# Feed-forward in pairs of tiles, half chunks turned as one, and norm, projection and merge joined to it

## The reference

```python
def fp4_quant_dequant(x):
    xb = x.reshape(shape[:-1] + (shape[-1] // BLOCK, BLOCK))
    scale = jnp.maximum(jnp.max(jnp.abs(xb), axis=-1, keepdims=True) / 6.0, 1e-12)
    idx = jnp.searchsorted(_MID, jnp.abs(xb / scale))
    return (_GRID[idx] * jnp.sign(xb / scale) * scale).reshape(shape)

def ffn(x, w_gate, w_up, w_down):                    # fp4_linear quantises both sides
    h = silu(fp4_linear(x, w_gate)) * fp4_linear(x, w_up)
    return fp4_linear(h, w_down)

x = x + 0.5 * ffn(layernorm(x), ...)
x = x + attention(layernorm(x), w_qkv, w_out)        # softmax(q k / 4) v, then w_out
x = x + 0.5 * ffn(layernorm(x), ...)
```

## Time and profile before

| | us |
|---|---|
| median of three runs | 4138.01 (4137.37 to 4140.72) |
| the profiled execution's own time | 4135.73 |
| its span, first to last instruction | 4133.9 |
| PE busy | 4009.2 (97%) |
| DVE busy | 3712.7 (90%) |
| ACT busy | 2450.9 (59%) |
| POOL busy | 1098.6 (27%) |

### The profile page before, as it was taken

One profiled execution on the slowest core, in us unless ns is written; L12 is line 12 of the kernel. 1 busy time (PEld: TensorE's weight loads), 2 busy tenths in 40 slices (PEclk: granted clock), 3 DMA queues, 4 the chain that ended last, 5 costly groups with the idle time before them and its releaser, 6 DMA issues. The chain is left out here.

```text
span 4133.9 us, 108840 instructions
## 1 busy us (share of the span) xinstructions
PE 4009.2 (97%) x46275; PEld 2314.2 (56%) x46275; DVE 3712.7 (90%) x6341; ACT 2450.9 (59%) x2770; POOL 1098.6 (27%) x1156
## 2 busy tenths in 40 slices
PE   3999998999999999999999999999999999899999
PEld 2777775568764444444444444444444443677776
DVE  7999983689999999999999999999999995799998
ACT  1222225467777777777777777777777778122222
POOL 3888872300000000000000000000000000288886
PEclk8999999999999999999999999999999999999999
DMA  3000002310010110001001001001100110100000
GB/s 134 1 1 1 1 1 99 122 58 29 21 40 20 30 31 29 21 27 34 25 25 34 26 21 39 21 29 31 29 21 29 31 29 5 34 16 16 16 16 21
DMA packets 77709, 125.57 MB, mean 30 GB/s; under 512 B 27688, under 2 KB 56744, under 8 KB 75432
## 3 DMA queue, kind: packets, MB, share of 16 engines
q1 hardware_dynamic: 77224, 118.62, 9.8%
HBM read 72.55 MB, written 36.31 MB: 26 GB/s over the span
## 5 line engine op out<-in xcount | busy, mean ns | idle before, releaser
L971 DVE TENSOR_REDUCE stats<-ps_b 128x1 f32<-128x512 f32 x4016 | 2488.7, 682 | 105.7 <-PE ps_b L1020 6.3
L958 ACT ACTIVATE probs<-ps_s 128x1024 f32<-128x1024 f32 x2048 | 1983.8, 1021 | 649.6 <-PE ps_s L1054 649.6
L1020 PE MATMUL ps_b<-w_ffn 96*32 96x512 bf16 x10688 | 1112.0, 382 | 6.2 <-PEq L653 5.9
L1032 PE MATMUL ps_o<-probs,w_qkvT 128*32 128x512 f32 x8192 | 1090.5, 592 | 0.6 <-ACT probs L958 0.6
L1054 PE MATMUL ps_s<-w_ffn 99*32 99x512 bf16 x10752 | 977.0, 380 | 0.5 <-ACT probs L958 0.5
L545 PE MATMUL ps_gu_f<-w_ffn,zT_f 128*128 128x352 f32 x2048 | 634.9, 463 | 10.3 <-DVE h_f L450 9.4
L1054 PEld LDWEIGHTS ps_s<-w_ffn 99*32 99x32 bf16 x10752 | 365.7, 98 | 377.4 <-issue 188.8
L1020 PEld LDWEIGHTS ps_b<-w_ffn 96*32 96x32 bf16 x10688 | 357.7, 96 | 376.7 <-issue 174.0
L1020 PE MATMUL ps_b<-K,Q 96*32 96x512 bf16 x5376 | 558.6, 381 | 0.2
L1054 PE MATMUL ps_s<-Q,K 99*32 99x512 bf16 x5632 | 508.8, 381 | 2.2 <-ACT probs L958 1.8
L545 PEld LDWEIGHTS ps_gu_f<-w_ffn,zT_f 128*128 128x128 f32 x2048 | 383.1, 192 | 204.8 <-ACT zT_f L402 11.9
(11 more groups left out here) (124 smaller groups left out, 3084.9 us busy)
## 6 DMA issues: line engine op xcount, KB each, us to landing
qk_parts_dram<-qk_parts SPq DMA_DIRECT2D x96, 256.0 KB, 2.9
w_ffn<-qk_parts_dram SPq DMA_DIRECT2D x84, 192.0 KB
w_ffn<-qk_parts_dram SPq DMA_DIRECT2D x84, 128.0 KB
x_res<-in_L_attn_x SPq DMA_DIRECT2D x4, 2048.0 KB, 19.6
factor<-denom_dram SPq DMA_DIRECT2D x64, 128.0 KB, 5.3
out<-x_res SPq DMA_DIRECT2D x16, 512.0 KB, 2.6
v_then_heads<-OT SPq DMA_DIRECT2D x224, 32.0 KB
w_ffn<-qk_parts_dram SPq DMA_DIRECT2D x84, 64.0 KB
```

Of the source, the lines that this page charges most:

```text
L958: nc.scalar.activation(probs[:, (2 * kt + half) % 4, :], ps_s[:, half, :], ACT.Exp, scale=float(DH) ** -0.5).then_inc(exped, 1)
L971: nc.vector.tensor_reduce(mx[:, s, k // 4, bass.ds(k % 4, 1)], ps_b[:, bank, :], AX.X, ALU.max).then_inc(bank_free, 1)
L1020: last = nc.tensor.matmul(ps_b[j:j + STRIP, bank, :], Q[s][0:PAIRS, qt * P + j:qt * P + j + STRIP], K[s][0:PAIRS, kb * 512:(kb + 1) * 512] ...
L1032: last = nc.tensor.matmul(ps_o[32 * c:32 * c + 32, :], V[s][:, kt, :], probs[:, (2 * kt + c // 2) % 4, (c % 2) * 512:(c % 2 + 1) * 512], s ...
```

## The change

In the feed-forward:

- Tiles are taken in pairs. hq and hT hold 2 x 704 = 1408 columns, 11 chunks without padding. Chunk 5 is shared: its rows 0 to 63 are the last 64 columns of the even tile, rows 64 to 127 the first 64 of the odd one. The even tile's h is turned as 5 chunks, the odd tile's as 6. The weights of the down product are laid out in 11 chunks to match, with five more pairs of transposes and copies in the weights stage and one small transfer.
- down(t) multiplies five whole chunks; for the odd tile two matmuls of 64 rows follow, one on each half of the array's rows, one into each tile's bank, and finish both tiles.
- LAG is 2. PE turns h of tile i-2 in step i, ahead of the gate/up products of tile i.
- On DVE the residual of tile i-3 now stands behind h of tile i, and for an even tile it waits for the down products of the odd tile after it; the statistics stand behind the block maxima.

Around it:

- The second norm is split: tiles 0 to 47 are done inside the first feed-forward (DVE behind steps 54 and 56, ACT behind step 55), and ACT prepares projection's first y there; tiles 48 to 63 are done inside projection. Projection starts with the q/k products of chunk 0, and turns chunk 1 only behind them.
- The merge is the head of the second feed-forward's block. It uses six banks of that stage. The norm of tiles 0 to 15 stands behind round 7, steps -4 to -1 of the feed-forward behind rounds 12, 15, 18 and 21, and the norm of the rest behind round 31.
- Several buffers share memory with others. Attention's instructions are the same.

```diff
-        AHEAD, LAG = 4, 3
+        AHEAD, LAG = 4, 2
...
+        def chunks(t):
+
+            return range(0, EVEN) if t % 2 == 0 else range(EVEN, PAIR)
...
-                    if old:
-                        dve.wait_ge(dn_done, i - LAG)
-                        nc.vector.scalar_tensor_tensor(out=m.x[:, i - LAG - 1, :], in0=ps_dn[:, q, 0:D], scalar=0.5 / SHRINK**2,
-                                                       in1=m.x[:, i - LAG - 1, :], op0=ALU.mult, op1=ALU.add).then_inc(x_done, 1)
...
-                    if old and out is None:
-                        dve.wait_ge(x_done, i - LAG)
-                        nc.vector.bn_stats(m.stats[:, i - LAG - 1, :], m.x[:, i - LAG - 1, :])
+                    if old:
+                        t = i - LAG - 1
+                        dve.wait_ge(dn_done, t + 2 - t % 2)
+                        nc.vector.scalar_tensor_tensor(out=m.x[:, t, :], in0=ps_dn[:, t % 2, 0:D], scalar=0.5 / SHRINK**2,
+                                                       in1=m.x[:, t, :], op0=ALU.mult, op1=ALU.add).then_inc(x_done, 1)
...
+                def turn_h(t):
+
+                    pe.wait_ge(hq_ready, t + 1)
+                    if t >= 1:
+                        pe.wait_ge(hT_kept, t)
+                    for k, c in enumerate(chunks(t)):
+                        last = nc.tensor.transpose(ps_hT[:, k * P:(k + 1) * P], hq[:, c * P:(c + 1) * P], m.ident[:])
+                    last.then_inc(hT_turned, 1)
+
+                def down(t):
+
+                    pe.wait_ge(hT_kept, t + 1)
+                    if t >= 2:
+                        pe.wait_ge(x_done, t - 1)
+                    whole = [c for c in chunks(t) if c != EVEN]
+                    for c in whole:
+                        last = nc.tensor.matmul(ps_dn[:, t % 2, 0:D], hT[:, c * P:(c + 1) * P], m.w_dnT[:, c, :],
+                                                start=(c == whole[0]), stop=False)
+                    if t % 2 == 1:
+                        for u in range(2):
+                            rows = slice(u * HALF_ROWS, (u + 1) * HALF_ROWS)
+                            last = nc.tensor.matmul(ps_dn[:, u, 0:D], hT[rows, EVEN * P:(EVEN + 1) * P], m.w_dnT[rows, EVEN, :],
+                                                    start=False, stop=True)
+                    last.then_inc(dn_done, 1)
...
+class NormAhead:
+
+
+    LO, HI = 0, 3 * KT
+    AT = HI + 6
...
+    def vector(self, dve, i):
+        if i == self.AT:
+            dve.wait_ge(self.norm.stats_in, self.HI)
+            self.norm.variance(dve, 0, self.LO, self.HI)
+        if i == self.AT + 2:
+            self.norm.finish(dve, 0, self.LO, self.HI)
...
+class Merge:
...
+    NORM_AFTER = PER_BATCH - 1
+    STEP_AFTER = {12: -4, 15: -3, 18: -2, 21: -1}
...
+    def wait_weights(self, pe):
+
+        pe.wait_ge(self.w_loaded, 16)
+        pe.wait_ge(self.x_done, self.NG)
```

More of the change, by code:

```diff
@@ L204, in weights_phase @@
         first_down = len(jobs)
[L205 to L207 removed]
+        for c in range(PAIR):
+            rows = P if c != EVEN else HALF_ROWS
+            lo = c * P if c <= EVEN else c * P - I
+            jobs.append(([dn3[:, j, lo:lo + rows] for j in range(KD)], m.w_dnT[0:rows, c, :], rows))
         with nc.Block() as block:
@@ L341, in ffn_phase, with normalise_chunk @@
+def normalise_chunk(nc, act, m, i):
+    for j in range(CHUNK):
+        t = i * CHUNK + j
+        last = nc.scalar.activation(m.y[:, j, :], m.x[:, t, :], ACT.Identity, bias=m.shift[:, t:t + 1], scale=m.rstd[:, t:t + 1])
+    last.then_inc(m.y_ready, 1)
+def ffn_phase(nc, m, tag, out, lead=None, tail=None):
     with ExitStack() as ctx:
@@ L417, in step @@
                         nc.scalar.activation(halves(silu[:]), gate, ACT.Silu, scale=1.0 / SHRINK).then_inc(silu_done, 1)
-                straight(step)
+                if lead is None:
+                    for i in range(-AHEAD, 0):
+                        at(step, i)
+                else:
+                    lead.scalar(act, lambda i: at(step, i))
+                for i in range(NT + LAG + 1):
+                    at(step, i)
+                    if tail is not None:
+                        tail.scalar(act, i)
             @block.vector
@@ L484, in step @@
                         nc.vector.tensor_tensor(hs[:, q, :], hs[:, q, :], hM[:, q, :], ALU.add).then_inc(h_step, 1)
-                straight(step)
+                if lead is None:
+                    for i in range(-AHEAD, 0):
+                        at(step, i)
+                else:
+                    lead.vector(dve, lambda i: at(step, i))
+                for i in range(NT + LAG + 1):
+                    at(step, i)
+                    if tail is not None:
+                        tail.vector(dve, i)
             @block.gpsimd
@@ L532, in step @@
                     if live(-LAG):
-                        pe.wait_ge(hq_ready, i - LAG + 1)
-                        if live(-LAG - 1):
-                            pe.wait_ge(hT_kept, i - LAG)
-                        for c in range(FC):
-                            last = nc.tensor.transpose(ps_hT[:, c * P:(c + 1) * P], hq[:, 1 - q, c * P:(c + 1) * P], m.ident[:])
-                        last.then_inc(hT_turned, 1)
+                        turn_h(i - LAG)
                     if live(0):
                         pe.wait_ge(zT_kept, i + 1)
+                        if first and lead is not None:
+                            lead.wait_weights(pe)
                         if live(-1):
@@ L655, in _, with high_part @@
             def _(act):
-                for i in range(-2, NC):
+                def high_part(i, q):
+                    if i >= 2:
+                        act.wait_ge(parts_stored[q], i // 2 * (16 * STORES))
+                    for n, (lo, hi) in enumerate(halves(i)):
+                        act.wait_ge(qk_done, i + n + 1)
+                        nc.scalar.copy(parts[q][0][:, lo:hi], ps_qk[:, lo:hi]).then_inc(high, 1)
+                        if i == END:
+                            act.wait_ge(rested, i + n + 1)
+                            nc.scalar.copy(parts[q][1][:, lo:hi], rest[:, lo:hi]).then_inc(middle, 1)
+                for i in range(-1, NC):
                     q = i % 2
+                    if i == 0:
+                        high_part(i, q)
+                    if i == ROOTS_AT:
+                        norm.roots(act, 1, 3 * KT, NT)
                     if 0 <= i + 1 < NC:
@@ new lines, with __init__, take_banks, bank @@
+    NORM_AFTER = PER_BATCH - 1
+    STEP_AFTER = {12: -4, 15: -3, 18: -2, 21: -1}
+    def __init__(self, nc, m, norm, ctx):
+        self.nc, self.m, self.norm = nc, m, norm
+        self.y_done, self.x_done, self.w_loaded = (ctx.enter_context(nc.semaphore(n)) for n in ("y_done", "x2_done", "ffn_w_back"))
+    def take_banks(self, banks):
+        self.banks = banks
+    def bank(self, i):
+        return self.banks[(i + 4) % len(self.banks)].rearrange("p (t d) -> p t d", t=self.G)
+    def wait_norm(self, act, tile):
+        act.wait_ge(self.norm.done, 1 if tile < KT else 2)
```

365 lines of the change are left out of this document (208 added, 157 removed).

## The result

The changed kernel takes **4298.3 us** (median; 4292.6 to 4307.8), the kernel before, on the same chip, 4139.4 us: **1.0385 times the time**, 95% interval 1.0368 to 1.0401, some 159 us slower. The forecast was 4225 with a range of 4150 to 4264. The direction was right; the time lies above the range. The profiled execution took 4301.5 us, its span is 4299.7.

A forecast was written before the change was run, and what follows sets the result against it. It took POOL's round with two DVE operations (8.34 us a tile) as the present bound, the two-round path after the change. Steady terms +52.8 and +45.9 with heads, ends and joins made +87.3 over 4135.73: 4223 profiled, 4225 for runs, range 4150 to 4264.

The forecast's parts named there:

- What bounds the kernel before: Feed-forward: POOL's round with two DVE operations sets 8.34 us a tile; PE is close behind, within some 0.2 us.
- The path over two rounds: Feed-forward, gate/up through quantised h to next gate/up: 18.45 us for two tiles in the first, 18.22 in the second.
- rival 1: Down products: halves not side by side, or switching the array costs; +0.43 us per pair, +27, 4252 us; chance 17%.
- rival 2: Feed-forward: wait for down products not on the path; 8.7 and 8.6 us per tile, 4162 us; chance 13%.
- rival 3: Feed-forward: two-round path does not bind, POOL's round sets 8.34 us again, joined stages stay as gain; 4123 us; chance 14%.
- rival 4: Feed-forward: PE's clock falls in the 2.3 us pause once per pair; at the worst 4327 us; chance 4%.
- at the worst: Upper price of PE's clock falling in the feed-forward pauses: 1.6 x 64 us on top, 4327 us.
- between gu(3) and gu(63): From tile 3's gate/up start to tile 63's: 60 steady tiles, +52.8 us in the first feed-forward, +45.9 in the second.
- The ends and the head with LAG 2: First feed-forward: head +2.9 us, end -1.8 and +2.7; second feed-forward: end +0.2.
- gu(63) to attention: From tile 63's gate/up start, first feed-forward, to attention's first table load: -7.5 us, with norm and projection start at -8.4.
- merge to gu(3): From the first merge product to tile 3's gate/up start, second feed-forward: -7 us, bounds 0 and -13.
- The norm operations fall where DVE waits for silu: 0: First feed-forward: norm operations moved behind steps 54 and 56 cost 0 us.

The follow-up runs named there:

- LAG 3 alone: The changed kernel with LAG 3 in place of 2, pairs, half products and joined stages kept: 4135.8 us, 0.9991 of the kernel before.
- the pause filled: The changed kernel with the two z transposes ahead of PE's wait for quantised h repeated eight times every second round: 4243.8 us, ratio 1.0256.
- the pause filled and a late norm: The changed kernel with z transposes repeated in PE's pause and the joined norm moved to the first feed-forward's end: 4242.5 us, ratio 1.0252.
- LAG 3 and POOL's order: The changed kernel with LAG 3 and POOL's scaled z of tile i+4 between the two h operations of tile i: 4113.1 us, ratio 0.9938.

## Why the prediction failed, point by point

**What bounds the kernel before**: POOL's round with DVE's part, 8.34. Borne out as far as tested: moving one POOL operation gave 8.21. That PE is next, "full to within some 0.2 us", is not shown: at 8.21 pairs with less PE work run no faster.

**The path over two rounds**: right, and close. Forecast 18.45 and 18.22 a pair; with the clock held up 18.53 and 18.33, and no piece of it is off by more than 0.10. LAG 3 alone takes the whole loss away.

**The half products** (rival 1): fell. 3.00 from down products to the residual for 2.90 forecast, where the rival has 3.33; they do lie side by side.

**The wait not on the path** (rival 2): fell, since the wait is 1.12 in the rows and moving it off the path gave 153 us. Its sum was tested too: 17.4 and 17.2 forecast for two rounds without it. Single tiles with LAG 2 took 17.42 and 16.90, but with another order on DVE, so the first agreement is in part luck; the change with the residual last took 16.90 twice.

**The path doesn't bind** (rival 3): fell. But 16.9 was named as the point where loss turns to nothing, and 16.90 is what comes out when the residual stands last: 4145, no gain and little loss.

**PE's clock falls in the pause** (rival 4): this is **the step that failed**. The pause was sized right (2.3 forecast, 2.09 measured for PE and 2.33 for its weight loads), but of "between these nothing is known" I made 4%, and a sum with no clock in it. In its place the runs show a clock that falls behind 26 of 30 such pauses in the first feed-forward and 7 of 30 in the second. The earlier trace rows shows the clock within a pause, where the change has 1.00 too; what bears on the question is the work behind it, and there the kernel before has the full clock:

```profile
92.66 4.97 PE L545 MATMUL ps_gu_f<-w_ffn,zT_f 128*128 128x352 f32 x16 [1.65 <-DVE h_f L450]
```

This full clock after 1.65 us idle and a fallen one after 3.08 bracket 2.3 about evenly; the case belonged in the range. Its price was 54.5 us in the runs (40 and 12 of it between gu(3) and gu(63)), about half of the 102 of "at the worst". With the pause filled the time is 4243.8, inside the range.

**The ends and the head with LAG 2**: the second failed step, some 17 us. The run with the pause filled and a late norm has a span 107.7 us over that of before where the sum said 87.3. gu(63) to attention is -0.7 for -7.5, merge to gu(3) -2.4 for -7, the end +5.6 for +0.2; the other 3.6 are spread over the rest.

The joins themselves came out: with LAG 3 alone gu(63) to attention is 239.1 us, 7.5 less than before, and merge to gu(3) 88.0, 7.2 less. Mis-sized were the terms beside them. For the end of the first feed-forward the sum had +0.9 (-1.8 and +2.7); in the filled run the last residual ends 27.6 us behind gu(63) for 21.1 before, +6.5. The end of the kernel had +0.2 and took +5.6. And merge to gu(0) is 59.9 us for 68.4, but gu(0) to gu(3) takes 33.0 for 26.9, since LAG 2 and the lower clock are felt at the head as well.

"The norm operations fall where DVE waits for silu: 0" was wrong: it counted DVE and forgot ACT, which waits for them and changes tables twice. They cost 3.7 us in the run with the pause filled and 9.05 with LAG 3 and POOL's order. At the end of the first feed-forward, the kernel after:

```profile
712.11 0.42 DVE L525 SCALAR_TENSOR_TENSOR x_res<-ps_dn_f,x_res 128x256 f32<-128x256 f32 x1 [3.50 <-PE ps_dn_f L628]
...
720.45 1.54 PE L613 MATMUL ps_T_f<-ident,v_then_heads 128*128 128x128 f32 x6 [5.37 <-POOL v_then_heads L595]
722.88 4.63 PE L623 MATMUL ps_dn_f<-w_ffn,hT_f 128*128 128x256 f32 x10 [0.89 <-ACT hT_f L472]
```

h of the last tile is late because DVE first waits 3.50 for the down products that the residual ahead of h's maxima needs, and what follows on PE runs at half clock (granted 0.50 from 720.4 on).

## What to carry to other kernels

When a change makes two dependent stages nearer neighbours (LAG 3 to 2), sum the path that loops through all engines before counting the busy time saved; here saved PE work was worth nothing and 0.1 us of path per tile is 13 us. Put an operation that waits for another engine behind everything of its own queue that somebody needs sooner: this one place was worth 153 us. A recurring pause of 2 us on PE had two prices here, its length and the slower clock behind it; a cheap test is to fill it with repeated work. Work out the ends of a pipeline as paths of their own: with a shorter lag they lost 6.5 and 5.6 us, where the steady pace said nothing.

## What the runs showed of the hardware beyond the expected

- Pauses of 2.09 us, once in 18 to 20 us in which PE is otherwise busy, let the clock fall from 2.4 to 1.2 GHz in 26 of 30 pairs; pauses of 1.90 in 7 of 30; a filled pause with 0.57 left in none. The fall is seen behind the pause, in some pairs from the transposes on (1.54 and 5.93 for 0.87 and 4.90), in most only in gate/up (6.59), and costs 1.7 us either way. Why some pauses of the same length have no fall is open.
- The change's four executions spread over 15 us, the longest (4307.8) at the lowest mean granted clock, 0.973, and the shortest (4292.6) at the highest, 0.979; with the pause filled four executions lie within 3.1 us.
- Adding 14 transposes a pair made the kernel 54.5 us faster.
- Of DVE's one-input operations on SBUF the TENSOR_SCALAR ones stretch beside POOL too: 0.93 for 0.51, 1.41 for 0.54, 1.42 for 0.26. The block maxima of h (TENSOR_REDUCE) take 0.88 beside POOL and without it. Moving work by a tenth of a microsecond changes which operation is hit; one such shift cost 0.68 us a pair in one feed-forward and nothing in the other.
